# Spreading the four dot fills of a tile among look-up steps on PE

## The reference

```python
e = jnp.stack([tbl_f[ids[:, f]] for f in range(26)], axis=1)          # (2048, 26, 128)
combined = jnp.concatenate([dense[:, None, :], e], axis=1)            # (2048, 27, 128)
interactions = jnp.einsum('bfd,bgd->bfg', combined, combined)
z = jnp.concatenate([dense, interactions[:, IU0, IU1]], axis=1)       # 128 + 351 columns
h = jnp.concatenate([z, dense], axis=1)                               # (2048, 607)
h = jnp.maximum(h @ W_top1 + b_top1, 0.0)                             # 512
h = jnp.maximum(h @ W_top2 + b_top2, 0.0)                             # 256
y = h @ W_top3                                                        # 1
```

## Time and profile before

| | |
|---|---|
| median of three runs | 381.35 us (380.23 to 384.43) |
| span of the profiled execution | 496.1 us (the profile gives no time of this execution beside the span) |
| PE matmul busy | 376.0 us, 3360 records |
| DVE, ACT, POOL busy | 244.4, 195.0, 254.8 us |
| mean granted PE clock | 0.904 of full speed |

### The profile page before, as it was taken

How to read it: one execution, slowest core, us unless ns; L and a number is a source line. 1 busy time by engine, 2 the same in 40 slices (tenths; PEclk the granted TensorE clock), 3 DMA queues, 4 the chain that set the end, 5 groups by cost and what they waited for, 6 DMA issues and landing times.

```text
span 496.1 us, 8109 instructions
## 1 busy us (share of the span) xinstructions
PE 376.0 (76%) x3360; PEld 301.4 (61%) x3360; DVE 244.4 (49%) x174; ACT 195.0 (39%) x261; POOL 254.8 (51%) x266
## 2 busy tenths in 40 slices
PE   1951777858586665978798796969788696879997
PEld 1630656647474554767586666867676455666787
DVE  4740789674919370765725750956566101112133
ACT  3810986414242521525252532434354334344400
POOL 6774540655737363646666554747466564730000
PEclk9985799989989796989998898989899898789899
DMA  8841763259915153456714533536232621123330
GB/s 210 218 134 41 218 187 85 70 156 275 227 29 161 45 155 103 109 150 153 183 46 128 160 87 104 143 93 193 74 89 63 168 73 27 49 63 100 69 71 5
DMA packets 38479, 58.44 MB, mean 118 GB/s; under 512 B 21665, under 2 KB 22561, under 8 KB 38444
## 3 DMA queue, kind: packets, MB, share of 16 engines
q1 hardware_dynamic: 29304, 40.74, 30.3%
q0 software_dynamic: 8192, 16.79, 13.5%
q10 hardware_dynamic: 948, 0.41, 0.4%
HBM read 47.68 MB, written 10.23 MB: 117 GB/s over the span
## 4 chain that ended last, share of the span: by engine, by line
PE 58%; issue 16%; DVE 11%; another core or an unknown queue 8%; SPq 3%; DMA 2%; ACT 2%; DVEq 0%; ACTq 0%
PE look_bank L727 25%; PE short_bank L821 15%; DVE one_hot L1031 8%; PE out_bank L757 6%; PE out_bank L771 4%; PE short_bank L806 4%; PE out_bank L766 3%; SPq L632 2%; DVE all_combined L1044 1%; DVE low_table L1019 1%; DMA spread_ids<-in_ids_by_feature 1%; PE out_bank L783 1%; SPq L621 1%; DMA last_scratch<-all_dots 1%
## 5 line engine op out<-in xcount | busy, mean ns | idle before, releaser
L682 POOL DMA_INDIRECT rows<-in_tbl,all_ids x256 | 253.9, 992 | 191.9 <-PE short_bank L821 81.9
L1031 DVE TENSOR_TENSOR one_hot<-spread_ids,row_bank 128x2048 fp32r<-128x2048 int32 (+3 forms) x80 | 170.7, 2175 | 27.1 <-PE look_bank L727 10.7
L727 PE MATMUL look_bank<-one_hot,high_table 125*128 125x512 f32 x328 | 140.8, 429 | 20.0 <-issue 16.1
L727 PE MATMUL look_bank<-one_hot,low_table 125*128 125x512 f32 x328 | 132.4, 404 | 0.6 <-issue 0.6
L821 PE MATMUL short_bank<-all_combined 128*59 128x54 f32 x2048 | 88.1, 247 | 53.2 <-issue 51.5
L821 PEld LDWEIGHTS short_bank<-all_combined 128*59 128x59 f32 x2048 | 79.7, 162 | 66.7 <-issue 66.5
L1044 DVE COPY all_combined<-short_bank 128x512 f32<-128x512 f32 x32 | 21.8, 691 | 156.2 <-PE short_bank L806 122.3
L727 PEld LDWEIGHTS look_bank<-one_hot,high_table 125*128 125x128 f32 x328 | 64.5, 197 | 40.5 <-issue 23.6
L727 PEld LDWEIGHTS look_bank<-one_hot,low_table 125*128 125x128 f32 x328 | 64.6, 197 | 16.9 <-issue 4.1
L925 ACT COPY all_dots<-short_bank 128x432 f32<-128x432 f32 x64 | 33.1, 518 | 97.1 <-remote 53.7
L878 ACT COPY looked_up<-look_bank 128x512 f32<-128x512 f32 x40 | 23.4, 586 | 120.8 <-remote 45.3
(11 more groups left out here) (42 smaller groups left out, 183.5 us busy)
## 6 DMA issues: line engine op xcount, KB each, us to landing
whole_table<-in_tbl SPq DMA_DIRECT2D x26, 448.0 KB
spread_ids<-in_ids_by_feature SPq DMA_DIRECT2D x40, 256.0 KB
block_scratch<-all_dots SPq DMA_DIRECT2D x24, 208.0 KB
rows<-in_tbl,all_ids POOLq DMA_INDIRECT x256
block_scratch<-all_dots SPq DMA_DIRECT2D x24, 104.0 KB
pairs<-block_scratch SPq DMA_DIRECT2D x72, 29.2 KB
whole_table<-in_tbl SPq DMA_DIRECT2D x26, 52.0 KB
whole_table<-in_tbl SPq DMA_DIRECT2D x2, 560.0 KB
```

Source lines behind the costliest of these rows:

```text
L682: nc.gpsimd.indirect_dma_start(rows[:, t % ROW_TILES, slot, :], None, tables[SLOT_FEATURES[slot]][:, :], bass.IndirectOffsetOnAxis(ap=all_ ...
L727: last = nc.tensor.matmul(look_bank[s % LOOK_BANKS][:], table_parts[part][TABLE_PLACE[s]][0:ROWS_K, c, :], one_hot[0:ROWS_K, (chunks_befor ...
L1031: last = nc.vector.tensor_tensor(one_hot[:, place:place + n, :], spread_ids[:, s % ID_PLACES:s % ID_PLACES + 1, :].to_broadcast([P, n, COLS]),
```

## The change

The diff does three things.

1. After each of the fills 0, 1 and 2 of a tile PE now runs two look-up steps of `work_after(t)`, which is one half. So six steps (three halves) stand between the fills, and are taken out of the steps after the turns. This holds for tiles 0 to 11, which have look-ups.
2. ACT's list of ends is changed with it: the look-ups that end between the fills stand after the end `("turn", t + 1, 0)`, which is after all four `copy_dots`, `copy_dense` and `move_looks`, and before the copies of turns 1 and 3. A look's high part moves with its copy.
3. DVE makes two of the tile's halves before the copies of the turns and not after them.

```diff
+BESIDE_FILL = 2
+
+HALVES_BEFORE_COPIES = 2
@@
-    return ahead + work_after(t)
+    return ahead + [step for step in work_after(t) if step not in BESIDE[t]]
+
+def steps_beside(t, b):
+
+    if b == FILLS - 1:
+        return []
+    return [step for step in work_after(t) if step[0] == "look"][BESIDE_FILL * b:BESIDE_FILL * (b + 1)]
+
+BESIDE = [[step for b in range(FILLS) for step in steps_beside(t, b)] for t in range(TILES)]
@@
-ENDS = [done_in(steps) for steps in STEPS]
+def ends_after(t):
+
+    ends, beside = done_in(STEPS[t]), done_in(BESIDE[t])
+    at = ends.index(("turn", t + 1, 0)) + 1 if beside else 0
+    return ends[:at] + beside + ends[at:]
+
+ENDS = [ends_after(t) for t in range(TILES)]
@@ dot_tile
                     last.then_inc(dots_done, 1)
+                    work(steps_beside(t, b))
@@ DVE
             for t in range(LAST * PER_BLOCK):
+                made = make(made, HALVES_BEFORE_COPIES)
                 for g in range(0, n_groups(t + 1), 2):
                     copy_group(t + 1, g)
                 if t > 0 and t % PER_BLOCK == 0:
                     low_inputs(t // PER_BLOCK - 1)
-                made = make(made, HALVES_AFTER[t // PER_BLOCK][t % PER_BLOCK])
+                made = make(made, HALVES_AFTER[t // PER_BLOCK][t % PER_BLOCK] - HALVES_BEFORE_COPIES)
```

## The result

The changed kernel takes 439.8 us in the median (438.6 to 441.8), the kernel before 382.1 us beside it: a ratio of 1.153 (95% interval 1.147 to 1.159). The forecast was 432 us, and slower.

The account below looks back on a forecast made before the run. PE was taken to bound the kernel, POOL near it. Median 381.35 us plus 3 (places), 38 (DVE's early halves), 8 (products), 1 (block end), 8 (clock), minus 7 (swallowed) gave 432 us, range 393 to 455.

Parts of the forecast that it names:

- turn 3 behind DVE's split: Tiles 1, 2, 5, 6, 9, 10: DVE's split awaits ACT's late high part, delaying turn 0's copy and PE: +38 us.
- products without cover: Tiles 4 and 8: first product comes straight after turn 3, before its inputs are done; 4.0 us each, +8 us.
- dots and look-ups changing places: PE, 36 new places where dots follow a look-up: 0.08 us each, the other way 0; +3 us.
- clock: PE idle 4 to 7 us in eight places, then at half rate: 1 us each, +8 us, ends 0 and 17.
- end of a block: Tiles 3, 7, 11: ACT copies the last looks later, before the next tile's dots: +1 us, 0 to 4.
- swallowed by waits of before: PE may already wait for POOL's rows in timed runs, which would hide part of the stalls: -7 us, ends 0 and -15.
- the faster rival: Gaps in PE's dots are real and look-ups between fills remove them: 361 us, chance 0.12.
- the same: POOL paces the timed run, so the stalls vanish in PE's waits for rows: 380 to 386 us, chance 0.08.
- POOL and the moved marks: Group 3 of each gather waits for a third fill some 3.7 us later; two tiles ahead, PE does not meet it late.

Follow-up runs that it names:

- before: The unchanged kernel, as seen in its repeat profile with no edit: 379.4 us, span 376.9 us.
- the second trace of before: The kernel before the change profiled once more, no edit: 379.4 us, span 376.9 us, next to no nameless idle.
- the first trace: The profile of the kernel before the change on which the prediction rests, of a rare long execution: span 496.1 us.
- the mended orders: The changed kernel with ACT's high parts made earlier, then further edits, tile 0's fills still apart: 398.4 us down to 384.9 us.
- an order that held POOL once for 5.6 us: The changed kernel reworked with one early high part (384.9 us), but all six look steps of a tile after fill 1: 385.4 us.
- both: Against the kernel before: fills apart in tiles 1, 2, 5, 6, 9, 10 only, one early high part, and SPLIT_WEIGHTS = 3: 381.8 us, ratio 1.007.

## Why the prediction was right, and where its terms were off

The prediction was right in sign, in size (432 for 439.8 us, range 393 to 455) and in its main step. That the total came so near is in part luck: places and clock were put 16 us too low together, and the swallowed waits, which are taken off, 8 us too low. The difference of the two spans, 61.0 us, by its terms:

| term | predicted | in the traces |
|---|---|---|
| turn 3 behind DVE's split, six tiles | 38 | 36.8 |
| products without cover | 8 (tiles 4, 8) | 6.3 + 2.7, and 2.4 more in tile 12 |
| dots and look-ups changing places | 3 | 36 x 0.30 = 10.8 |
| clock | 8 | 16 to 17 |
| end of a block | 1 | 0.2 |
| swallowed by waits of before | -7 | -14, and -1 at the fills |

**The stall before turn 3** was read from the code and priced from one stretch: 5.25 and 7.5 us a tile, measured 4.9 and 7.3 to 7.45. It appears in the six tiles named and in no other. That moving ACT's high parts alone removed it (398.4 us), and moving DVE's split alone as well (403.4 us), shows the cause.

**The products** waited 9.0 us in tiles 4 and 8 for 8 forecast, 6.3 and 2.7 us where 4.0 each was taken, and in part for another reason. The working had the inputs ready as long after the dots as in before; in tile 4 ACT itself stood 2.9 us for the pair loads. Timeline of ACT in the changed kernel:

```profile
154.37 0.43 ACT L929 COPY all_combined<-dense_cols 128x128 f32<-128x128 f32 x1
157.68 0.62 ACT L972 CAST high_dense<-dense_cols 128x512 fp32r<-128x512 f32 x1 [2.88 <-DMA pairs<-block_scratch]
```

The prediction called SP's orders unchanged and looked at its loads of tables and ids alone. It left out the pairs: they hang on the end of a block's last dots, which now lies some 10 us after their start and not 3.7. This also cost the 2.4 us of tile 12, which the prediction took as unchanged (4.04 us in before, 6.39 after). Leaving those tiles alone brought it back to 4.2.

**A place between fills** costs 0.30 us and not 0.08. The way from look-up to dots was right (0.32 us against 0.23), but I gave the way back nothing. Timeline of PE in the changed kernel:

```profile
60.32 1.08 PE L842 MATMUL short_bank<-all_combined 128*59 128x54 f32 x32 [1.42 <-ACT all_combined L919]
61.33 0.50 PE L748 MATMUL look_bank<-one_hot,high_table 125*128 125x512 f32 x1
61.67 0.40 PE L748 MATMUL look_bank<-one_hot,low_table 125*128 125x512 f32 x1
61.91 0.40 PE L748 MATMUL look_bank<-one_hot,high_table 125*128 125x512 f32 x1
```

The second look-up starts 0.34 us after the first, where 0.23 us is the median within a kind, and the first comes 0.15 us after the last dot, against 0.027 us from dot to dot in the mean. With the medians of all 36 places: (0.148 - 0.027) + (0.335 - 0.227) + (0.318 - 0.227) - 0.020, as the first two dots come 7 ns apart, is 0.30 us. Tile 0, whose only wait is the 1.4 us before its dots in either kernel, grew by 1.3 us for three places, 0.4 us more than this gives; that rest is open.

**The clock** was put at half of what it cost. Windows over the nine stretches at 0.50, its 1.2 GHz level, in the changed kernel (us, then PE busy; first, second and sum):

```profile
95.80:99.20 3.40, 3.40 (x11) 2.81 (x12) 3.40 (x3) 0.68 (x1) 1.84 (x2) 0.50 0.70 180
116.30:126.50 10.20, 5.44 (x15) 4.48 (x16) 9.52 (x7) 3.31 (x5) 4.09 (x5) 0.50 0.15 37
...
sum 64.60, PE 41.88 PEld 33.98 DVE 52.62 ACT 21.65 POOL 30.46; mean PE 4.65 PEld 3.78 DVE 5.85 ACT 2.41 POOL 3.38
```

and the sum of the two such stretches of before:

```profile
sum 10.30, PE 8.84 PEld 7.25 DVE 4.05 ACT 2.97 POOL 7.86; mean PE 4.42 PEld 3.62 DVE 2.02 ACT 1.49 POOL 3.93
```

Busy at half rate for 41.9 us loses 20.9 us, 8.8 us lose 4.4: 16.5 us more. A second number agrees: PE does the same 3360 matmuls in both kernels and is busy 361.7 us in the change and 334.3 us before, 27.4 us more, which is the 10.8 us of the places and the 16.5 us of the clock. Each of the nine waits of 2.7 us and more before turns and products has such a stretch with it, 2.3 us lost on average, where one row had shown 2.1 and I took 1. In the second trace of before, full clock holds through every unbroken stretch of dots, and its two half-clock stretches lie at waits of 3.1 and 4.0 us before a turn and a product. So the fills needed no look-ups for the clock's sake: the faster rival was read from a disturbed trace. The Trainium skill, "Perfetto Trace Analysis", Matmul Optimizations, says that the matmul engine scales its power with its use. This case agrees, but the waits that the change brought, and not the dots, are where the clock sank: 0.50 in nine stretches beside nine waits.

**Swallowed waits.** PE's 14.5 us before turns in before, behind DVE, ACT and rows, are nearly all gone in the change: the 37.3 us are the stalls and one of 0.5. POOL shows the same from its side. Its waits for PE went from 2.1 to 61.2 us. These 59 us are near the 61 us of the spans, but the two are not the same sum: the 256 gathers themselves took 7.2 us less (254.7 for 261.9 us) and the steps between them 3.7 us less, so the last gather starts 48.1 us later (390.0 for 341.9), and 12.9 us were added behind it. In before POOL had no slack; in the change PE was the slower, and POOL waited for it. The prediction had POOL in a rival that needed PE waits of 4 us in each of eight tiles for "the same"; PE waited 5.4 us for rows in all, so the stalls could not vanish there. That POOL never waits in before could not be seen in the first trace, where PE's idle had drawn POOL's waits with it.

**POOL and the moved marks** was half right. PE never waited for rows in the change. But group 3's later mark did hold POOL, 4.2 us in tile 0, where the prediction counted on gathers being two tiles ahead. In the change the stalls hide it; in the mended orders it stayed.

Summed: 36.8 + 0.5 - 14.5 before turns, 11.4 before products, -1 at the fills, 10.8 and 16.5 give 60.5 of 61.0 us. That before's waits also differ a little from run to run (379.4 here, 382.1 in the comparison) stays within 3 us of it.

## What to carry to other kernels

When work is put in front of a copy on an in-order engine, follow what that work itself waits for through the other engines' orders: a split that needs another engine's late step turns a cheap prefetch into a stall of everything behind it. When steps are moved between two ends, also ask who takes the second end as its start, here the stores and loads of pairs. And before PE's order is tuned, look whether another queue never waits: POOL issued gathers without a break from 3 to 342 us, no order of PE's steps ended that sooner, and an order that held POOL once for 5.6 us paid 5.9 us at the end.

## What the runs showed of the hardware that was not expected

One execution can differ from the rest so far that its profile misleads: 496.1 us of span against 376.9, with 51.5 us of nameless idle within dots, against 1.0 us of it in the second trace. Its durations of single ACT and DVE instructions were right all the same (a copy of ten looks 2.46 us, against 2.37 to 2.44 in the changed kernel, a high part 1.08 against 1.05, a copy of a turn 0.69 in both traces of before); its gaps and its clock (0.904 against 0.985) were not. Why that execution was so slow is open; no run here was made for it. The timed run of 487.3 us had a mean granted clock of 0.655. Length and clock need not go together: one of the twelve runs of "both" took 1086.8 us at a granted clock of 1.0, also unexplained.

A gather of 128 rows kept POOL for 0.94 us in the median and the next one, where it waited for nothing, began 0.30 us after its end, in every trace here. From the first of 256 to the last that would be 317 us; longer gathers, up to 2.0 us, made it 339 us in before.
